# Graph network of four layers on one core: weight product moved behind the sum, residual product moved beside a sweep, batch statistics about a pivot, last norm on ScalarE

## What is computed

```python
x = _layernorm(x + L0(x))     # attention over in- and out-edges
x = _layernorm(x + L1(x))     # two typed attention layers (hgt)
x = _layernorm(x + L2(x))     # graph convolution
x = _layernorm(x + L3(x))     # mean of edge messages, two products, batch norm

# L2
dinv = jnp.where(deg > 0, jax.lax.rsqrt(deg), 0.0)
norm = dinv[src] * dinv[dst]
h = x @ W
agg = segment_sum(h[src] * norm[:, None], dst) + b
return jnp.where(agg >= 0, agg, 0.1 * agg) + x

# L3
message = x[src] + (edge_attr @ edge_w + edge_b)
aggr = segment_sum(message, dst) / jnp.maximum(cnt, 1.0)[:, None]
h = (1.0 + eps[0]) * x + aggr
out = jax.nn.relu(h @ w1 + b1) @ w2 + b2
out = out + (x @ res_w + res_b)
mean = jnp.mean(out, axis=0)
var = jnp.var(out, axis=0)
return jax.nn.relu((out - mean) * jax.lax.rsqrt(var + BN_EPS) * gamma + beta)
```

## Time and profile before

| what | value |
|---|---|
| time before, median of 3 runs | 8809.26 us (8806.7 to 8819.43) |
| the profiled execution's own time | 8815.13 us |
| its span in the trace | 8813.4 us |
| POOL busy | 6086.1 us (69%) |
| VectorE busy | 5593.5 us (63%) |
| ScalarE busy | 3091.3 us (35%) |
| TensorE busy | 2052.3 us (23%) |

### The profile page before, as it was taken

One profiled execution on the slowest core, in us unless ns is written; L12 is line 12 of the kernel. 1 busy time (PEld: TensorE's weight loads), 2 busy tenths in 40 slices (PEclk: granted clock), 3 DMA queues, 4 the chain that ended last, 5 costly groups with the idle time before them and its releaser, 6 DMA issues. The chain is left out here.

```text
span 8813.4 us, 60467 instructions
## 1 busy us (share of the span) xinstructions
PE 2052.3 (23%) x16367; PEld 1898.9 (22%) x16367; DVE 5593.5 (63%) x10159; ACT 3091.3 (35%) x3341; POOL 6086.1 (69%) x6351
## 2 busy tenths in 40 slices
PE   5776634555400000810000720000500000300002
PEld 5666634555300000710000610000400000200002
DVE  7665546766599998868888468888632222432225
ACT  6333312333266665345555345555200000100002
POOL 2777777777777775667776367777267776577773
PEclk5555555555555555955555865555555555555556
DMA  4621114444366665656665556666333332233331
GB/s 131 216 60 42 37 51 134 130 133 135 115 204 219 218 216 180 206 195 216 216 216 201 170 192 216 216 216 211 93 95 105 105 105 95 78 106 105 105 105 56
DMA packets 496250, 1288.01 MB, mean 146 GB/s; under 512 B 153909, under 2 KB 262024, under 8 KB 428968
## 3 DMA queue, kind: packets, MB, share of 16 engines
q1 hardware_dynamic: 236712, 755.83, 24.3%
q0 software_dynamic: 229248, 473.78, 18.5%
q10 hardware_dynamic: 29952, 54.54, 2.4%
HBM read 731.68 MB, written 551.98 MB: 146 GB/s over the span
## 5 line engine op out<-in xcount | busy, mean ns | idle before, releaser
L1405 POOL DMA_INDIRECT l_swp_G<-table,KVI x1664 | 1576.4, 947 | 512.3 <-issue 506.7
L1661 POOL DMA_INDIRECT l2s_G<-table,OTHI x832 | 786.7, 946 | 388.1 <-issue 253.3
L1661 POOL DMA_INDIRECT l3s_G<-table,OTHI x832 | 787.7, 947 | 301.5 <-issue 253.3
L1065 POOL DMA_INDIRECT arrived<-plc_QS,plc_idx x832 | 812.3, 976 | 253.5 <-issue 244.3
L1065 POOL DMA_INDIRECT slots<-REC,plc_idx x832 | 798.5, 960 | 273.1 <-issue 251.7
L1150 POOL DMA_INDIRECT l_G<-table,OTHI x832 | 790.1, 950 | 256.1 <-issue 253.0
L904 PE MATMUL plc_pr<-plc_seen,plc_otf 128*128 128x49 f32 x3328 | 861.5, 414 | 12.4 <-DVE plc_seen L674 12.4
L904 PEld LDWEIGHTS plc_pr<-plc_seen,plc_otf 128*128 128x128 f32 x3328 | 846.6, 326 | 32.1 <-issue 31.9
L1508 DVE SCALAR_TENSOR_TENSOR l_swp_QS<-l_swp_QS,KEEP,l_swp_QX 128x128 f32<-128x128 f32 x1664 | 588.3, 354 | 45.9 <-DMA l_swp_QX<-queries 8.6
L1617 PE MATMUL l_swp_AW<-l_swp_ET,ones 128*128 128x512 f32 x4 | 4.1, 1140 | 2155.2 <-DVE l_swp_ET L1597 2155.2
L1287 DVE TENSOR_TENSOR_SCAN l_X<-l_AW,l_X 128x2244 f32<-128x2244 f32 x104 | 502.5, 4831 | 3.6
(11 more groups left out here) (491 smaller groups left out, 9633.2 us busy)
## 6 DMA issues: line engine op xcount, KB each, us to landing
sums<-l_ROW SPq DMA_DIRECT2D x104, 1088.0 KB, 4.6
l_swp_QX<-queries SPq DMA_DIRECT2D x104, 1088.0 KB, 8.3
sums<-l_swp_ROW SPq DMA_DIRECT2D x104, 1088.0 KB, 5.2
queries<-plc_zrow SPq DMA_DIRECT2D x55, 1088.0 KB
plc_QX<-queries SPq DMA_DIRECT2D x104, 544.0 KB, 4.2
l_A<-arrived SPq DMA_DIRECT2D x52, 1056.0 KB, 7.7
sums<-l3s_ROW SPq DMA_DIRECT2D x52, 1032.0 KB
plc_low<-low_rows ACTq DMA_DIRECT2D x208, 256.0 KB, 3.6
```

The source lines that it names most:

```text
L1065: pool.indirect_dma_start(out=slots, out_offset=bass.IndirectOffsetOnAxis(ap=idx[:, c % IB, j:j + 1], axis=0), in_=g.REC[:, c * CH + j, :] ...
L1405: pool.indirect_dma_start(out=G[:, c % GR, j, :], out_offset=None, in_=table, in_offset=bass.IndirectOffsetOnAxis(ap=index[:, c * CK + j:c ...
L1661: pool.indirect_dma_start(out=G[:, c % GR, j, :], out_offset=None, in_=table, in_offset=bass.IndirectOffsetOnAxis(ap=g.OTHI[:, c * CK + j: ...
```

## The change

**Attention stages.** The gather and scatter of `first` at the end of t0 and t1 go. Each attention sweep issues one gather of the queries (`own`) ahead of its edge gathers, and VectorE's query 0 becomes a wait for it and a copy.

```diff
@@ attention_sweep, POOL and VectorE
+            pool.indirect_dma_start(out=own[:, :], out_offset=None, in_=g.queries,
+                                    in_offset=bass.IndirectOffsetOnAxis(ap=g.SEGI[:, k, :], axis=0)).then_inc(taken, 16)
             for c in range(NCK):
...
-            v.memset(QS[:, QH - 1, :], 0.0)
...
-                if n and j == 0:
+                else:
+                    v.wait_ge(taken, 16)
+                    v.tensor_copy(QS[:, 0, :], own[:, 0:D]).then_inc(q_ok, 1)
+                    return
@@ turn_layer, POOL
-                passed()
-                pool.indirect_dma_start(out=first[:, :], ... in_=g.queries, ...).then_inc(taken, 16)
-                pool.wait_ge(taken, 16)
-                passed()
-                pool.indirect_dma_start(out=g.queries, ..., in_=first[:, :], in_offset=None).then_inc(back, 16)
-                pool.wait_ge(back, 16)
```

```diff
@@ turn_layer, gcn
-    LAG = 11 if gcn else 3
+    LAG = 2 if gcn else 3
...
-            def own_rows(n):
-                v.wait_ge(made2, n + 1)
-                v.tensor_scalar(g.OWN[:, n, :], pg[:, 0:D], g.DINV[:, n:n + 1], None, ALU.mult).then_inc(owned, 1)
+                elif j == 3:
+                    v.tensor_tensor(g.OWN[:, group(G), :], x, cols3(g.DINV[:, group(G)]).to_broadcast(wide), ALU.mult).then_inc(owned, 1)
@@ turn_plain, VectorE
+            def middle(G):
+                v.wait_ge(kept, (G + 1) * GT)
                 link(v.scalar_tensor_tensor(out=y, in0=y, scalar=0.1, in1=y, op0=ALU.mult, op1=ALU.max))
...
+            first(0)
             for G in range(NG + 1):
+                if G + 1 < NG:
+                    first(G + 1)
                 if G < NG:
-                    first(G)
+                    middle(G)
                 if G >= 1:
                     second(G - 1)
@@ turn_plain, ScalarE
+            for n in range(NB + 1):
+                if n < NB:
+                    copy(n)
+                if n >= 1:
+                    keep(n - 1)
+                G = n // GT - 1
+                if n % GT == 4 and 0 <= G < NG - 1:
+                    close(G)
+                    if G >= 1:
+                        root(G - 1)
```

```diff
-                    before = S[:, b, j - 1, :] if j else ROW[:, 1 - b, CK - 1, 0:D]
-                    after = S[:, b, j, :] if j < CK - 1 else ROW[:, b, CK - 1, 0:D]
+                    before = S[:, b, j - 1, :] if 0 < j <= SP_ else ROW[:, b if j else 1 - b, (j - 1) % CK, 0:D]
+                    after = S[:, b, j, :] if j < SP_ else ROW[:, b, j, 0:D]
```

```diff
+            def part(G):
+                if G == 0:
+                    v.wait_ge(pivoted, 1)
+                    link(v.tensor_scalar(stat[:, 0, :], pp[:, 0:D], -1.0 / (GT * P), None, ALU.mult))
+                v.tensor_tensor(HH[:, group(G), :], HH[:, group(G), :], flat(stat[:, 0, :]), ALU.add).then_inc(parted, 1)
...
             for s_ in range(-3, NB):
                 if 0 <= s_ + 1 < NB:
                     keep(s_ + 1)
+                if s_ >= GT and (s_ + 1) % GT == 1 and s_ // GT - 1 < NG - 1:
+                    part(s_ // GT - 1)
                 mix(s_ + 3 + GT)
...
+            def total(G):
+                pe.wait_ge(squared, G + 1)
+                for n in range(G * GT, (G + 1) * GT):
+                    pe.matmul(pm[:, 0:D], ones_of(n)[:, :], HH[:, n, :], start=(n == 0), stop=(n == NB - 1))
+                    o = pe.matmul(pv[:, 0:D], ones_of(n)[:, :], SQ[:, G % 2, n % GT, :], start=(n == 0), stop=(n == NB - 1))
+                o.then_inc(totalled if G < NG - 1 else varied, 1)
```

```diff
             def first(G):
-                if G == 0:
-                    v.wait_ge(squared, NG)
+                if G >= 2:
+                    v.wait_ge(normed, (G - 1) * GT)
...
-                link(v.tensor_scalar(m[:, 0, :], m[:, 0, :], -1.0 / D, None, ALU.mult))
-                v.tensor_tensor(x, x, cols3(m[:, 0, :]).to_broadcast(wide), ALU.add).then_inc(centered, 1)
+                v.tensor_scalar(m[:, 0, :], m[:, 0, :], -1.0 / D, None, ALU.mult).then_inc(centered, 1)
...
-                v.tensor_tensor(x, x, cols3(m[:, 2, :]).to_broadcast(wide), ALU.mult).then_inc(normed, 1)
+                v.tensor_tensor(m[:, 3, :], m[:, 0, :], m[:, 2, :], ALU.mult).then_inc(scaled, 1)
```

More of the change, by code:

```diff
@@ L37 @@
 QB = 3
+SP_ = 12
 BIG = 1.0e30
@@ L1751, in _, with residual @@
         def _(pe):
+            def residual(n):
+                pe.wait_ge(copied, n + 1)
+                if n >= 1:
+                    pe.wait_ge(kept, n)
+                pe.matmul(pb[:, 0:D], xt[:, n % 2, :], wr[:, :], start=True, stop=False)
+                pe.matmul(pb[:, 0:D], g.ones[0:1, :], br[:, 0, :], start=False, stop=True).then_inc(made, 1)
+            if weight:
+                pe.wait_ge(joined, 1)
+                for n in range(NB):
+                    if n >= 1:
+                        pe.wait_ge(copied, n)
+                    pe.transpose(pt[:, 0:P], g.X[:, n, :], g.ident[:, :]).then_inc(turned, 1)
+                    if n >= 1:
+                        residual(n - 1)
+                residual(NB - 1)
             pe.wait_ge(rowed, NCK)
```

221 lines of the change are left out of this document (103 added, 118 removed).

## The result

The changed kernel takes 8795.19 us (median of 20 runs, 8790.97 to 8800.02) against 8806.97 us (20 runs) for the one before: a ratio of 0.9986, 95% interval 0.9979 to 0.9992. It is faster by some 12 us, less than 0.2%. The profiled execution has a span of 8794.7 us, 18.7 less than that of before.

A forecast was written before the change was run, and what follows sets the result against it. POOL's gather issue bounds the sweeps, so only stages between them and sweep edges can move. Terms -7.0 - 34 - 4 - 0.6 + 1 + 22 + 8 = -14.6; 8815.1 - 14.6 - 5.9 = 8795 us, range 8770 to 8826.

The forecast's parts named there:

- Attention stages: Ends of t0 and t1: barrier waits of 4.6 and 4.9 us go, each sweep gains a 1.25 us gather; -7.0 us.
- t2: Stage t2: shorter tiles and groups, and one wide product behind the last scaling; -34 us, from -46 to -26.
- The tail: End of t2: the new OWN is one wide product, 1.13 us behind the last scaling; 9.65 us less.
- The -6.4 for the first group: First group of t2, run in part at 2.4 GHz: about 0.9 us saved for each of seven tiles.
- The -18.2 for the five groups: Five groups of t2: 20.4 us each where they took 24.0; 18.2 us saved.
- t3: Stage t3: residual product's passes move inside a chain of 12.65 us a group; -4 us, from -9 to +3.
- Sweeps: Sweeps: shorter last ScalarE copy -0.6 us, VectorE's two-SBUF links +1 us (0 to +31), residual tiles in l3s nothing.
- The rival of blocked gathers: Sweeps: VectorE's two-SBUF links block a gather in every chunk, +31 us instead of +1, total 8825 us; chance 0.07.
- t4, statistics: t4's batch statistics: part, square and total inside the mix loop lengthen groups; +22 us.
- The clock term: t4's statistics: PE's clock falls in each group until the total; +22 us, against +12 at 2.4 and +42 at 1.2 GHz.
- t4, last norm: t4's final loop: VectorE's next first step waits for ScalarE's norm, 10.0 us a group; +8 us, from -2 to +11.
- the pair of ScalarE's blocks: t4's final loop: seven squares take 1.93 us and seven norms 2.56 us a group, without overlap.

The follow-up runs named there:

- u_own: Changed kernel with only the first query's gather and scatter put back at the end of t0 and t1; ratio 1.0017 to the kernel before.
- x_best2: Changed kernel with the old batch statistics, seven row statistics, last loop's root first, t3's square and root one tile earlier; ratio 0.9960 to the kernel before.
- u_sp15: Changed kernel with 15 columns in PSUM again in the convolution's sweep l2s alone; ratio 1.0007 to the kernel before.
- x_spread: Changed kernel with PE's block of 14 sums dealt out, two in each of the next seven tiles; ratio 0.9966 to the kernel before.
- x_late: Changed kernel with ScalarE's square and PE's block of sums in t4 one tile later; ratio 0.9975 to the kernel before.
- x_ring: Changed kernel with last-loop row statistics for all seven groups instead of two; ratio 0.9969 to the kernel before.

## Why the prediction was right, point by point

**Attention stages**, -7.0 forecast: -3.8 and -5.7, of which 1.4 is the spread of the sweep between them, so -8.1. The barrier's wait of SP was the right row: the removed chain ended last, and in the changed kernel SP's wait at the end of t0 is 0.2 us where it was 4.6. u_own shows the cause for both stages (5.7 or more, and 4.4 to 4.6).

**t2**, -34 forecast, -32.2 measured (-30.4 to -34.1 with the same t2 in the other runs on ordinary chips). The new group took 20.8 where 20.4 was worked out; the tile took 2.26 instead of 2.14, and in it PE waits 0.2 to 0.3 us for VectorE. The tail came as forecast: last norm to last OWN one wide step. The sum is nearer than its terms. The -6.4 for the first group was wrong: the first norm starts 39.8 us into the stage (39.3 before) and the second 19.4 us behind it (20.0 before), so nothing is gained there. The -18.2 for the five groups was too small: they took 97.8 us from norm to norm instead of 120.2, or -22.4, above all because the last one takes 14.8 us and not 20.4. The two errors nearly cancel, and that is luck.

**t3**, -4 forecast, -4.2 measured; 12.63 us a group against 12.65. The chain sum, turn, product, keep, four tiles, root, scaling is the one that the trace shows, VectorE's 1.28 us for the root included; x_best2 shows by experiment that this wait is in the chain (11.63 with the root a tile earlier).

**Sweeps**, +1 and -0.6: the gathers' mean did not move (947 to 945 ns), the copy took 1.45 us as forecast, l3s hid the residual tiles. The rival of blocked gathers is settled by u_sp15 and by the gathers themselves: at these lengths (0.35 us) and this phase 2 of 81 are lengthened by 0.08 us and a few by 0.01 to 0.03. The rule of the Trainium skill (SBUF — State Buffer, "Who interferes with whom"), by which a VectorE instruction with two SBUF inputs contends with a GpSimd instruction that reads SBUF, agrees with the traces, for the wide operations (1.82 us, 1.51, 1.25) and for the short links (1.02).

**t4, statistics**, +22 forecast, +25.5 measured. The step "PE can't reach the tiles behind the total, and the next mix waits for those" was right (x_spread, without the block, takes 21 us off). The clock term was chosen between two worked bounds, +12 and +42, and not worked out; that it came near is in part luck. The prediction put the fall at "each part and square", but had the total end it. Measured, the clock falls in the total itself or just ahead of it, behind an idle of 2.8 us that the prediction did not have in its chain: ScalarE's square waits for VectorE's part with the next tile's copy behind it. x_late cuts that idle to 1.5, moves the block by a tile, and 14 us go; which of the two does it, and whether the idle is the cause of the fall, no run separates. The groups lay between the two bounds: 13.7 us, with 11.5 at full and 15.7 at half clock. At full clock a group takes 10.93 (x_late). And the loss is not where the prediction had it: +19.3 us come before the last group's first mix step and +6.1 behind it, where the prediction had nothing at full clock.

**t4, last norm**, +8 forecast, +9.7 measured. The mechanism was right (x_ring takes the wait out, with ScalarE's work unchanged, and the loop falls to 59.8). The term that was too small is the pair of ScalarE's blocks: 2.15 instead of 1.93 for the squares and 2.80 instead of 2.56 for the norms. Of these 0.46 us a group 0.25 arrived (10.25 against 10.0), since the hand-overs were shorter than estimated. The norm with two pointer operands took 480 ns (0.387 to the next), where the step from one row gave 0.46 and 0.35. The Trainium skill (ScalarE: Activation LUTs, "What ACT_TABLE_LOAD costs") gives 93 ns for each pointer, and the estimate by it is 0.48 and 0.39: here its figure was nearer than mine.

By these terms the sum is -9.3 instead of -14.6; the rest of the profiled difference of -18.7 comes from stretches that the change doesn't touch. The medians moved by -11.8 us (interval of the ratio: -18 to -7). The forecast started from a median of three runs, 8809.3, and the median of twenty is 8807.0; with a difference 2.8 us too large from a start 2.3 us too high, the 8795 hit 8795.2. That is luck. The forecast of "within 0.2%" rested on gains of 46 us and losses of 31, measured as some 44 and 35, and both sides were shown by taking them apart.

## What to carry to other kernels

Work that is spread into an in-order pipeline costs what stands behind it: here 2.8 us of idle and a block of 28 passes per group, to save one stretch of 16 us at the end (8732.8 to 8748.5 before). Deal such a block out over the tiles, and put an engine's new wait behind the short operations that others wait for. When work goes to an idle engine, look at the buffer that then ties the two together: a ring of seven small statistics instead of two turned a loss of 9.7 us into a gain of 5, and the root ahead of the squares made it 8.6.
